# Reordering the work beside the first block's units in a fused Mamba2 and ternary FFN kernel

## The reference

```
xn = layernorm(x)
xz = xn @ in_proj_w.T;  x_branch, z = split(xz)
x_branch = silu(causal_conv4(x_branch) + conv_b)
X, dt, B, C = split(x_branch @ x_proj_w.T)       # 16 heads of 64, state 128
dt = softplus(dt @ dt_proj_w.T + dt_proj_b);  A = -exp(A_log) * dt
Y = ssd(X * dt, A, B, C) + X * D                 # chunked scan with a running state
attn = (Y * silu(z)) @ out_proj_w.T
q(w) = clip(round(w / (mean(|w|) + eps)), -1, 1) # ternary weights
ffn = (sigmoid(xn @ q(w1).T) * (xn @ q(w2).T)) @ q(w3).T
return x + attn + ffn
```

## Time and profile before

| | |
|---|---|
| time before, median of 3 runs | 1608.19 us (1607.5 to 1609.03) |
| the profiled execution | 1608.5 us, its span 1606.4 us |
| mean granted TensorE clock | 0.990 of full speed |
| PE busy | 1556.3 us, 97% of the span |
| DVE busy | 1173.1 us, 73% |
| ACT busy | 888.1 us, 55% |
| POOL busy | 550.7 us, 34% |

### The profile page before, as it was taken

The page is one execution under the profiler, slowest core; times in us unless marked ns, Lnnn a source line. Parts: engine busy times, 40 slices in busy tenths (PEclk is TensorE's granted clock), DMA queues, the critical chain, the costliest instruction groups (busy, mean ns, idle before and its releaser), DMA issues.

```text
span 1606.4 us, 25318 instructions
## 1 busy us (share of the span) xinstructions
PE 1556.3 (97%) x9086; PEld 743.1 (46%) x9086; DVE 1173.1 (73%) x1820; ACT 888.1 (55%) x1840; POOL 550.7 (34%) x536
## 2 busy tenths in 40 slices
PE   7779899999999999999999999999999999999999
PEld 3334444444444444444444444444444444444444
DVE  7978886688576885688856887568866688576762
ACT  6787536565456644566455663646535565356641
POOL 3116674343034422154222441325403343034310
PEclk9899999999999999999999999999999999999999
DMA  7155430233302433033321334113350233402420
GB/s 268 42 183 170 144 107 27 55 104 86 72 28 74 103 88 60 34 86 92 88 45 48 87 91 101 18 61 92 86 99 19 65 103 77 82 27 74 97 68 27
DMA packets 228605, 131.66 MB, mean 82 GB/s; under 512 B 175200, under 2 KB 176992, under 8 KB 228480
## 3 DMA queue, kind: packets, MB, share of 16 engines
q1 hardware_dynamic: 228480, 130.05, 30.3%
HBM read 100.38 MB, written 29.62 MB: 81 GB/s over the span
## 4 chain that ended last, share of the span: by engine, by line
PE 78%; DVE 7%; issue 4%; ACT 4%; DMA 2%; POOL 2%; SPq 1%; POOLq 0%; DVEq 0%; ACTq 0%
PE bank L614 16%; PE bank L724 13%; PE bank L508 9%; PE bank L744 9%; PE bank L524 8%; PE bank L697 8%; PE bank L534 5%; PE bank L646 3%; PE bank L658 2%; PE bank L631 2%; ACT edc L988 2%; POOL less L1730 1%; DMA xin<-x_squares 1%; PE bank L561 1%; DVE edc L1368 1%
## 5 line engine op out<-in xcount | busy, mean ns | idle before, releaser
L614 PE MATMUL bank<-wx_hi,arena 128*128 128x512 f16 x1024 | 318.6, 381 | 0.0
L724 PE MATMUL bank<-xt_hi,q 128*128 128x512 f16 x704 | 267.3, 380 | 0.0
L724 PE MATMUL bank<-xt_lo,q 128*128 128x512 f16 x704 | 267.3, 380 | 0.0
L614 PE MATMUL bank<-wx_lo,arena 128*128 128x512 f16 x512 | 195.2, 381 | 0.0
L1701 POOL TENSOR_TENSOR mdc<-edc,mdc 128x512 f16<-128x512 f32 x56 | 64.8, 1156 | 299.8 <-ACT mdc L1000 299.8
L744 PE MATMUL bank<-q,arena 128*128 128x512 fp8e4 x704 | 162.4, 379 | 0.0
L988 ACT ACTIVATE edc<-csl,csv 128x128 f32<-128x128 f32 x512 | 155.8, 389 | 0.7 <-DMA csl<-sums 0.7
L614 PEld LDWEIGHTS bank<-wx_hi,arena 128*128 128x128 f16 x1024 | 100.7, 98 | 114.1 <-issue 2.5
L1368 DVE TENSOR_TENSOR edc<-edc,gt 128x512 f32<-128x512 f32 x128 | 110.5, 902 | 56.7 <-ACT edc L993 56.6
L1027 ACT CAST arena<-full 128x512 f16<-128x512 f32 x88 | 54.3, 617 | 146.9 <-DVE full L1447 146.9
L1719 POOL TENSOR_TENSOR xin<-xin,xs 128x512 f32<-128x512 f32 x60 | 76.7, 1278 | 154.4 <-DVE xin L1391 154.4
(11 more groups left out here) (218 smaller groups left out, 3520.9 us busy)
## 6 DMA issues: line engine op xcount, KB each, us to landing
csl<-sums SPq DMA_DIRECT2D x128, 256.0 KB, 3.7
y_squares<-xs SPq DMA_DIRECT2D x56, 256.0 KB, 2.0
xin<-y_squares SPq DMA_DIRECT2D x168, 64.0 KB, 2.5
xin<-x SPq DMA_DIRECT2D x32, 256.0 KB, 3.9
res<-x SPq DMA_DIRECT2D x32, 256.0 KB, 3.1
out<-res SPq DMA_DIRECT2D x32, 256.0 KB, 2.0
raw<-w_ffn SPq DMA_DIRECT2D x25, 256.0 KB, 2.9
x_squares<-mdc SPq DMA_DIRECT2D x24, 256.0 KB, 2.0
```

The lines of the kernel that those rows point to most:

```text
L614: i = pe.matmul(banks[0][:], act[:, k, c * P:(c + 1) * P], wt[:, k, hf * half:(hf + 1) * half], start=(n == 1), stop=(n == 3 * ki))
L724: i = pe.matmul(up_bank(b, m, j)[:], q12[:, j, m, k, :], part[:, k, :], start=(n == 1), stop=(n == 2 * kd))
```

## The change

Only block 0 changes. In a unit u of block 0:

- DVE makes Y of unit u (`scan`) ahead of decay(u+1), not behind it and an `aside()`.
- On DVE xdt and xdt_lo of unit u+1 now follow decay(u+1) at once; the two `aside()` calls that stood ahead of them come behind xdt_lo and behind xst_lo.
- The residual sum (`attn`) of units 2, 4 and 6 stands between xdt and xdt_lo, not behind xst_lo.
- On ACT `xs` of unit u+1 comes directly behind decay(u+1); one `aside()` lies between it and xdt_hi, one between xdt_hi and xst_hi.
- On POOL the first `aside()` comes behind `y_skip`, and the third behind project_x(u+1).
- On SP the load of the residual rows comes ahead of the unit's loads of pieces.

```diff
 # SP
+                    if u and u % 2 == 0:
+                        load_res(b, u // 2 - 1)
                     for _ in range(4):
                         aside()
-                    if u and u % 2 == 0:
-                        load_res(b, u // 2 - 1)
...
 # ACT
                 act.mul(xs[u % 2][:], banks[0][:], unscale).then_inc(S["xs"], 1)
+                between()
                 act.wait_ge(S["xdt"], at(b, "xdt", u))
...
-                    aside()
-                    aside()
                     if u + 1 < len(units):
-                        project_x(b, u + 1)
+                        project_x(b, u + 1, aside)
+                        aside()
                         if goes_on(b, u + 1):
                             update(b, u + 1)
+                    else:
+                        aside()
+                        aside()
...
 # DVE
+                    if b == 0:
+                        scan(b, u)
                     if u + 1 < len(units):
                         decay(b, u + 1)
                     if u == 0:
                         project_z(b, 1)
-                    aside()
                     if b and u == 7:
                         ffn_up(b, 0)
-                    scan(b, u)
+                    if b:
+                        scan(b, u)
+
+                    def attention():
+                        if b == 0 and u and u % 2 == 0:
+                            project_out(b, u // 2 - 1)
+
+                    if u + 1 < len(units):
+                        project_x(b, u + 1, attention)
                     aside()
-                    if u + 1 < len(units):
-                        project_x(b, u + 1)
...
-                    if b == 0 and u and u % 2 == 0:
-                        project_out(b, u // 2 - 1)
+                    aside()
...
 # POOL
                     if has_state(b, u):
                         if goes_on(b, u):
                             before_chunk(b, u)
-                    aside()
                     if has_state(b, u):
                         scan(b, u)
                     aside()
...
                         project_x(b, u + 1)
+                    aside()
                     aside()
```

More of the change, by code:

```diff
@@ L940, in project_z, with project_x @@
                                scale=0.5 / (XN_SCALE * W_SCALE)).then_inc(S["z_tanh"], 1)
-            def project_x(b, u):
+            def project_x(b, u, between=lambda: None):
                 act.wait_ge(S["x_mm"], at(b, "x_mm", u))
```

## The result

| | before | after |
|---|---|---|
| median of 5 runs | 1608.19 us (1606.82 to 1609.03) | 1615.09 us (1614.85 to 1616.42) |
| profiled execution, span | 1608.5, 1606.4 us | 1616.42, 1614.3 us |
| mean granted clock | 0.990 | 0.989 |

A forecast was written before the change was run, and what follows sets the result against it. DVE's order holds PE in units 0 to 3, DVE's work in 4 and 5; about 21 us could be gained. Late loads eat the gains: plus 1.6 us on 1608.5 gives 1610.1, said as 1610.0, range 1602 to 1614.

The forecast's parts named there:

- the named places: ACT waits for DMA 2 us and more at about 98, 110, 115 and 182 us.
- One sign: Unit 1: the transpose on PE would no longer wait for Y, a wait of 2.7 us before.
- plus 1.4 us: Unit 1: PE's first projection waits for yt_lo(1) until 119.25, 1.4 us later than before.
- DVE does O4 at once, until 109.35: Unit 1: DVE's piece O4 follows xdt_lo(2), costed at 0.6 us; O7's load then leaves at 109.4.
- counted in nothing: Residual load ahead of the pieces: 1 us of traffic ahead of M8, given no cost.
- upper bound: Unit 1: O7's and M8's loads both take 5.2 us; PE waits until 121.7, plus 3.8 us.
- The sum: Main case: B1 0.9 us late, whole kernel 1.6 us slower at 1610.1, said as 1610.0; chance 0.48.
- rival 2: Unit 5: the 3.3 us wait at B1 lets the clock fall, PE loses 3.4 us: 1613.5; chance 0.22.
- scan(7) 181.05: Unit 7: scan(7) starts on PE at 181.05 instead of 184.8, a gain of 3.7 us.
- Y ahead of the decay: Unit 1: Y fits into DVE's wait for exp and alone gives back up to 2.7 us of the transpose.
- POOL's move: POOL's new order lies under the waits named; no cost of its own.
- ACT's move: ACT puts two pieces between xs and xdt_hi, of which 0.3 us shows.

The follow-up runs named there:

- e16: Changed kernel with POOL's multiply by D cut to 8 columns in block 0: 1613.4 against 1609.6 us for the kernel before.
- e10: Changed kernel with one of DVE's two pieces ahead of xdt again in units 0 and 1 alone: 1609.7 us, kernel before 1608.8.
- e11: Changed kernel with one of DVE's two pieces ahead of xdt again in units 2 to 7 alone: 1613.4 us, kernel before 1608.8.
- e1: Kernel before with only Y moved ahead of the decay on DVE in block 0: 1610.8 against 1608.9 us.
- e6: Kernel before with only the residual loads moved ahead of the unit's loads of weights: 1608.9 against 1608.0 us.
- e15: e9 with POOL's order of before alone, ACT's staying new: 1606.8 us against 1609.6 for the kernel before.
- e14: e9 with ACT's order of before alone, POOL's staying new: 1613.1 us against 1609.6 for the kernel before.
- e9: Changed kernel with one DVE piece ahead of xdt, residual loads behind the weights, S1 right behind xst_lo in unit 5: 1606.4 us, kernel before 1608.0.
- e17: Changed kernel with one DVE piece ahead of xdt, S1 right behind xst_lo, residual rows asked for one place earlier still: 1607.6 us, kernel before 1609.6.

## Why the prediction was wrong

**The mechanism was right in the main.** ACT waits for loads at the named places, at two of them under the 2 us named (1.74 and 1.47), and once more for 3.36 us in unit 0; the residual sum no longer holds PE; scan(2) waits over 5 us for xdt_lo; PE stands 3.16 us at B1 for S1, where 3.3 were forecast. From decay(2) to xdt_lo(2) are 7.1 us, forecast 7.3. One sign failed: the transpose of unit 1 still waits 2.16 us for Y.

**Unit 1 was mis-sized, and it is the step that failed.** The working ended it with "plus 1.4 us" at the first projection; measured are plus 3.8. The first projection hangs on M8's load. It was to leave at 111.6 and left at 114.02, 2.4 us later, and M8 was on ACT 4.9 us behind it, so the load itself was not sized too small. Two things kept it back:

- DVE was later. "DVE does O4 at once, until 109.35" became 110.98. Of these 1.6 us some 0.7 came with xdt_lo(2), since decay(2) started at 101.58 and not at 100.5 (there, too, a piece, O0, had taken 1.53 us). The other 0.9 are O4's piece, costed at 0.6 us from rows in which POOL was idle. e16 shows that this is POOL's multiply.
- SP was later. O5's piece, which M8's load waits for, ended at 112.78. But SP was until 114.02 behind M7 (1.18 us to issue, 0.43 before), csl and the residual row. The forecast had no term for the queue, and the residual load was "counted in nothing".

How the 2.4 us divide between the two is not shown: with the multiply away (e16) the load left earlier, but took longer. e10 shows what the moved pieces of units 0 and 1 cost together, 5.1 us. The prediction's upper bound has the measured numbers, 121.7 and plus 3.8 us, but by chance: it took O7's load at 5.2 us, and O7 was on ACT 2.8 us behind its load, as in the earlier trace rows.

The stretched piece could have been priced. The earlier trace rows shows xdt_lo(2) at 0.97 us beside POOL, and the prediction itself counted a slow decay "beside a busy POOL", but not a slow piece.

The Trainium skill, SBUF — State Buffer, section Who interferes with whom, has the rule that was not used: a DVE instruction with two inputs in SBUF (the memory of all tiles but the banks) contends with a GpSimd instruction that reads SBUF, and contention there is an exclusive lock. The trace agrees for POOL's multiplies: the piece ends 0.55 us behind the multiply, while the copy of the state out of its bank, with no second input in SBUF, took 0.68 us beside it. It does not agree for POOL's compare: T4 in the changed kernel started at 157.20, beside a compare of POOL that ran from 156.04 to 157.60, and took 0.74 us, as T10 did at 188.11 with POOL idle.

**The late time was passed on.** The sum let B1 be 0.9 us late. 3.3 us came: 2.4 us more than worked out entered at unit 1, and 2.2 more arrived at B1 (in e10 5.1 and 5.3 us less).

**The clock at B1** was rival 2, with a chance of 0.22. It happened in the profiled execution and cost 1.7 us of unit 6 (6.86 us for X instead of 5.18), half of the 3.4 us that the rival had. Its condition, "the 3.3 us at B1 let the clock fall", held in four of the seven profiles with such a wait. The forecast's 1610.1 with this rival's 3.4 us is 1613.5, still 1.6 us under what was measured.

**Units 6 and 7.** "scan(7) 181.05" was 185.64, late by B1 (2.2), the clock (1.7) and 0.7 us between the projection and scan(7), where xdt_lo(7) took 1.35 us beside POOL instead of 0.95. From there to B2 were 6.8 us instead of 6.0: T9, too, took 1.53 us behind POOL, and ACT waited 3.78 us for M32. The residual sum's 4.1 us were gained as forecast and lost again between the transpose of unit 6 and B2. Half level then lasted to 198 us, forecast 192.7. The last projection is 7.2 us late, where the sum had 1.6; in e11 it is 4.4 us earlier, 1.7 of it by the clock, which held there at B1.

**Y ahead of the decay** was said to give back up to 2.7 us. e1 shows that alone it gives nothing: xdt(2) then waits for xs on ACT.

**The residual load**, "counted in nothing", costs ACT 2.2 us in e6, but the time under 1 us. **POOL's move** was rightly counted as nothing (e15, with one of DVE's pieces ahead of xdt). **ACT's move** was treated as 0.3 us; e14 shows it is what makes DVE's move pay.

The loss was not inevitable. One piece ahead of xdt, one behind xst_lo, and S1 early give 0.15% less than before (e9, e15, e17: 2.2 to 2.6 us by the ratios). What stays open is why the clock falls in one profile and holds in another after the same wait.

## What to carry to other kernels

A piece moved off the path of one engine is not free if a load waits for it: follow each moved instruction to the buffer that it frees, the queue that refills it, and the engine that reads it next. Cost a moved instruction by what runs beside it in its new place, not by its row in the old one. And two engines that hand a value back and forth need their orders moved together: ACT's part of this change saves 5 to 6 us beside DVE's, while ACT's and POOL's parts without DVE's cost some 3.6.

## What was not expected of the hardware

A DVE instruction with both inputs in SBUF stood until a POOL multiply was done: 1.53 us instead of 0.68 to 0.74, five times for a piece in block 0, and 0.69 us for O4 with the multiply cut away. A compare of POOL did not hold such a piece (0.74 us).

The granted clock after the same wait differs between profiles. At B1, with 3.0 to 3.3 us of standing, it fell to half level in four profiles and held in three; each fall costs 1.7 to 2.9 us. That is of the size by which the executions of one kernel differ, some 4 us, but no kernel was profiled twice to show that it is the cause.
